# A recurrence with gates over 2,048 tokens: inner products of keys and queries formed per head in a stage of their own and laid out by DMAs

## The reference

```python
def step(St, inp):
    kt, qt, vt, at, bt = inp
    Sk = jnp.einsum('bhij,bhj->bhi', St, kt)
    err = Sk - vt
    Sn = at[..., None] * St - (bt[..., None] * err)[..., None] * kt[:, :, None, :]
    ot = jnp.einsum('bhij,bhj->bhi', Sn, qt)
    return (Sn, ot)
_, outs = jax.lax.scan(step, S0, (tfirst(k), tfirst(q), tfirst(v), tfirst(a), beta.transpose(1, 0, 2)))
```

## Time and profile before

| what | value |
|---|---|
| median of 3 runs | 9,737.57 us |
| lowest, highest | 9,728.86, 9,740.81 us |
| the profiled execution's own time | 9,730.12 us |
| its span, first to last instruction | 9,728.3 us |
| PE busy, share of the span | 7,968.3 us, 82% |
| PEld busy | 4,939.8 us, 51% |
| DVE busy | 5,028.8 us, 52% |
| ACT busy | 2,588.3 us, 27% |
| POOL busy | 2,232.0 us, 23% |
| mean granted clock of PE | 0.687 of full speed |

### The profile page before, as it was taken

The page is one execution under the profiler, slowest core; times in us unless marked ns, Lnnn a source line. Parts: engine busy times, 40 slices in busy tenths (PEclk is TensorE's granted clock), DMA queues, the critical chain, the costliest instruction groups (busy, mean ns, idle before and its releaser), DMA issues. The chain is left out here.

```text
span 9728.3 us, 83645 instructions
## 1 busy us (share of the span) xinstructions
PE 7968.3 (82%) x25042; PEld 4939.8 (51%) x25042; DVE 5028.8 (52%) x7386; ACT 2588.3 (27%) x4982; POOL 2232.0 (23%) x1657
## 2 busy tenths in 40 slices
PE   3888598888899898889978989695452888899799
PEld 2766355555555555555544568542221772222387
DVE  3888544444444444444456643226878773333322
ACT  1232222222222222222223421114442113333111
POOL 0545533333333333333311111010000000000011
PEclk6999755555555555555569989896565558888799
DMA  4343322222222222222221110221110221111200
GB/s 144 127 144 130 105 61 61 61 61 61 61 61 61 61 61 61 61 61 61 61 91 61 48 48 26 101 77 44 30 33 7 62 51 39 35 35 27 94 20 30
DMA packets 635607, 612.38 MB, mean 63 GB/s; under 512 B 457888, under 2 KB 537248, under 8 KB 594080
## 3 DMA queue, kind: packets, MB, share of 16 engines
q1 hardware_dynamic: 635408, 610.13, 21.7%
HBM read 447.65 MB, written 162.40 MB: 63 GB/s over the span
## 5 line engine op out<-in xcount | busy, mean ns | idle before, releaser
L1349 PEld LDWEIGHTS scan_pq<-scan_ring,scan_Ssb 128*128 128x128 f32 x4064 | 911.6, 330 | 296.1 <-issue 296.1
L887 POOL TENSOR_TENSOR ffn_hid_low<-ffn_hid,ffn_hid_high 128x512 fp32r<-128x512 f32 x128 | 164.6, 1286 | 3561.5 <-ACT ffn_hid_high L877 3561.5
L1349 PE MATMUL scan_pq<-scan_ring,scan_Ssb 128*128 128x32 f32 x4064 | 931.8, 399 | 0.0
L297 PE MATMUL proj_acc<-proj_xn,proj_w 128*128 128x512 f32 x3072 | 728.9, 400 | 125.1 <-ACT proj_decay L343 90.9
L2242 PE MATMUL attend_ot<-attend_e,attend_v 128*64 128x512 f32 (+3 forms) x1280 | 679.3, 620 | 91.7 <-ACT attend_e L2269 91.7
L297 PEld LDWEIGHTS proj_acc<-proj_xn,proj_w 128*128 128x128 f32 x3072 | 593.7, 194 | 260.4 <-ACT proj_decay L343 93.8
L1866 PE MATMUL csum_sc<-csum_qk 96*128 96x512 f32 (+3 forms) x640 | 288.4, 567 | 395.5 <-ACT csum_e L1890 350.1
L390 DVE SCALAR_TENSOR_TENSOR proj_y<-proj_raw,proj_cw,proj_y 128x2048 f32<-128x2048 f32 x144 | 574.6, 3990 | 19.1 <-DVE proj_y L386 2.6
L1206 ACT ACTIVATE scan_uT<-scan_turn 64x128 f32<-64x128 f32 x384 | 104.1, 271 | 1698.8 <-PE scan_turn L1360 1698.8
L1254 PE MATMUL scan_work<-scan_gram,scan_ones 128*128 128x512 f32 x512 | 523.1, 1125 | 34.2 <-ACT scan_kT L1220 29.4
L1421 POOL TENSOR_TENSOR scan_gram<-scan_ring,scan_gram 128x512 f32<-128x512 f32 x64 | 96.8, 1513 | 1873.7 <-ACT scan_gram L1161 1873.7
(11 more groups left out here) (238 smaller groups left out, 15730.3 us busy)
## 6 DMA issues: line engine op xcount, KB each, us to landing
scan_abar<-decays SPq DMA_DIRECT2D x128, 1024.0 KB, 4.7
csum_qk<-qk SPq DMA_DIRECT2D x96, 256.0 KB
cmax_qk<-qk SPq DMA_DIRECT2D x96, 256.0 KB
attend_qk<-qk SPq DMA_DIRECT2D x96, 256.0 KB
proj_beta_rows<-beta SPq DMA_DIRECT2D x16, 1024.0 KB, 8.2
stream_k<-proj_res SPq DMA_DIRECT2D x16, 1024.0 KB, 3.9
stream_beta_k<-proj_resb SPq DMA_DIRECT2D x16, 1024.0 KB, 3.9
stream_beta_v<-proj_resb SPq DMA_DIRECT2D x16, 1024.0 KB, 3.8
```

The source lines that it names most:

```text
L297: mm = pe.matmul(acc[:, (j * TT + t) % 8, :], w[:, u, wh, j, k, :], xn[:, xh, k, t * TOK:(t + 1) * TOK], start=(p == 0 and k == 0), stop=( ...
L887: pool.tensor_tensor(hid_low[:, x % 2, :], hid[:, x % 2, :], hid_high[:, x % 2, :].bitcast(F32), ALU.subtract).then_inc(low_done, 1)
L1349: last = pe.matmul(pq[:, nu % 2, :, h, :], Ssb[:, q, g, e, :], ring[:, 0:2, h, nu * C:(nu + 1) * C], start=(q == 0 and g == 0 and e == 0), ...
```

## The change

A new stage, gram_phase, runs between block_decay_phase and scan_phase. For each head it multiplies, with the contraction over the 128 key dimensions, each window of 128 tokens of KK with the same window and the 16 tokens behind it of KB and QQ (288 columns), and turns the window of KK. ACT and VectorE copy the results to SBUF, and SP stores the diagonal parts (16 rows each) to `band` and the turned keys to `kT_dram` in HBM. It also writes zeros into three small tensors in HBM, `xz`, `uz` and `dots`.

In the scan, gram_next, turn_k, gram_first, gram_rest, the eight ones matmuls, their copies and masks are taken out, and so are the seven staging products on GpSimd. In their place SP packs from `band`: pack_dots writes the products inside subblocks to `dots` (28 DMAs per chunk), and build writes those inside a block to `uz` and those across blocks to `xz` (24 DMAs per chunk), each at its place of a matrix that is otherwise zero. load_dots, load_grams and load_keys bring them to SBUF. ACT negates the part of dots that belongs to KB (negate), in block v = 0 of each chunk. The decays are no longer in the ring but in `avec`, one buffer; dots has one buffer too. oring now holds pairs of blocks and is stored every second block. pq is ordered by head, then KB or QQ.

The updates are 128, 256 and 128 columns wide: update 0 reaches only the second subblock; update 1 reaches the third and fourth and carries the first two subblocks' results together (128 rows, the first one scaled by carry_first); update 2 as before.

The diff, cut to the new functions and the order of the work:

```diff
+def gram_phase(nc, streams, band, kT_dram, padded, ident, T):
+    W = T // P
+    SPAN = P + C
+    with ExitStack() as ctx:
+        m = Memory(nc, ctx, "gram")
+        keys = m.sb("keys", [P, 2, T])
+        both = m.sb("both", [P, 2, 2, T + C])
+        tile = m.sb("tile", [P, 2, W, GH + 1, 2, C])
+        kt = m.sb("kt", [P, 2, W, P])
+        zero = m.sb("zero", [P, 2048])
+        idt = m.sb("ident", [P, P])
+        g_ps = m.ps("g", [P, 2, 2, 512])
+        t_ps = m.ps("t", [P, 2, 4, P])
...
+    def load(h, u):
+        one = lambda s: streams[s][bass.ds(h, 1)].rearrange("o p t -> p (o t)")
+        sp.dma_start(keys[:, u, :], one(KK)).then_inc(k_in[u], 16)
+        sp.dma_start(both[:, u, 0, 0:T], one(KB)).then_inc(both_in[u], 16)
+        sp.dma_start(both[:, u, 1, 0:T], one(QQ)).then_inc(both_in[u], 16)
+    def store(i, u):
+        h = i * 2 + u
+        sp.wait_ge(gram_even, (h + 1) * (W // 2))
+        sp.wait_ge(gram_odd, (h + 1) * (W // 2))
+        rows = band[bass.ds(h, 1)].rearrange("o b s w r x -> b s (o w) (r x)")
+        for k in range(GH):
+            sp.dma_start(rows[k], tile[C * k:C * (k + 1), u, :, k:k + 2].rearrange("p w r q t -> p w (r q t)")).then_inc(band_out[u], 16)
+        sp.wait_ge(turn_copied, (h + 1) * TURNS)
+        keys_by_block = kT_dram.rearrange("(w k g) p j -> k (g p) w j", k=GH, g=2)
+        for k in range(GH):
+            sp.dma_start(keys_by_block[k, bass.ds(h * C, C)], kt[C * k:C * (k + 1), u]).then_inc(kt_out[u], 16)
+    sp.dma_start(idt[:, :], ident).then_inc(ident_in, 16)
+    load(0, 0)
+    load(1, 1)
+    sp.wait_ge(zeroed, 3)
+    for flat in padded:
+        sp.dma_start(flat, zero[:, 0:flat.shape[1]]).then_inc(padded_out, 16)
+    def turn(i, more):
+        for u in range(2):
+            store(i, u)
+            if more:
+                load(i * 2 + u + 2, u)
+    run_all(sp, H // 2, turn)
...
+            for w in range(W):
+                if not (isinstance(i, int) and i == 0 and u == 0 and w < 4):
+                    n = h * (W // 2) + w // 2
+                    if w % 2 == 0:
+                        pe.wait_ge(gram_even, n - 1)
+                    else:
+                        pe.wait_ge(gram_odd, n - 1)
+                pe.matmul(g_ps[:, w % 2, (w // 2) % 2, 0:2 * SPAN].rearrange("p (q t) -> p q t", q=2), keys[:, u, w * P:(w + 1) * P],
+                          both[:, u, :, w * P:w * P + SPAN], start=True, stop=True).then_inc(gram_done, 1)
+                if w % 4 == 3:
+                    g = h * TURNS + w // 4
+                    if not (isinstance(i, int) and i == 0 and u == 0 and w // 4 < 2):
+                        pe.wait_ge(turn_copied, g - 1)
+                    for v in range(w - 3, w + 1):
+                        last = pe.transpose(t_ps[:, (w // 4) % 2, v % 4, :], keys[:, u, v * P:(v + 1) * P], idt[:, :])
+                    last.then_inc(turn_done, 1)
+    run_turns(pe, H // 2, turn)
...
+            for w in range(0, W, 2):
+                act.wait_ge(gram_done, h * W + w + 1)
+                act.activation(tile[:, u, w].rearrange("p r q t -> p q r t"),
+                               g_ps[:, 0, (w // 2) % 2, 0:2 * SPAN].rearrange("p (q r t) -> p q r t", q=2, t=C),
+                               ACT.Copy).then_inc(gram_even, 1)
+                if w % 4 == 2:
+                    act.wait_ge(turn_done, h * TURNS + w // 4 + 1)
+                    act.activation(kt[:, u, w - 2:w + 2], t_ps[:, (w // 4) % 2], ACT.Copy).then_inc(turn_copied, 1)
+    run_turns(act, H // 2, turn)
...
+            for w in range(1, W, 2):
+                dve.wait_ge(gram_done, h * W + w + 1)
+                dve.tensor_copy(tile[:, u, w].rearrange("p r q t -> p q r t"),
+                                g_ps[:, 1, (w // 2) % 2, 0:2 * SPAN].rearrange("p (q r t) -> p q r t", q=2, t=C)
+                                ).then_inc(gram_odd, 1)
+    run_turns(dve, H // 2, turn)
...
+    def load_kq(it, half):
+        for w in (RK, RQ):
+            load(w, it, half, kq_in[half])
+    def load_a(it, half):
+        sp.dma_start(avec[:, :, :, :].rearrange("p h n s -> p h (n s)"),
+                     streams[3][:, :, bass.ds(it * RING + half * CHUNK, CHUNK)]
+                     .rearrange("h p t -> p h t")).then_inc(a_in, 16)
+    def pack_dots(it, half):
+        for v in range(BPC):
+            at0 = band[:, BPC * half + v, 0, bass.ds(it, 1), 0]
+            for q, row in ((1, 0), (1, 1), (1, 2), (1, 3), (0, 0), (0, 1), (0, 2)):
+                first = row + 1 - q
+                n = 4 - first
+                place = 4 * row if q else 13 + 3 * row
+                rows = bass.AP(band.tensor, at0.offset + row * TROW + q * C + first, [[HROW, H], [4 * TROW + 4, 4], [1, n]])
+                out = bass.AP(dots.tensor, half * DOTS * U + (4 * v) * DOTS + place, [[SPC * DOTS, H], [DOTS, 4], [1, n]])
+                sp.dma_start(out, rows, allow_slow_non_contiguous=n == 1).then_inc(packed[half], 16)
+    def load_dots(it, half):
+        sp.wait_ge(packed[half], 16 * 7 * BPC * (it + 1))
+        sp.dma_start(gram[:, :, :].rearrange("p u x -> p (u x)"), dots[half:half + 1, :].to_broadcast([P, DOTS * U])).then_inc(dots_in, 16)
+    def build(it, half):
+        for v in range(BPC):
+            rows = band[:, BPC * half + v, :, bass.ds(it, 1)].rearrange("h s o r x -> h (s o) r x")
+            zbase = (half * BPC + v) * XZ
+            sp.dma_start(bass.AP(xz.tensor, zbase, [[C * 256 + 2 * C, H], [256, C], [1, 2 * C]]), rows[:, :, 1, :]).then_inc(built[half], 16)
+            ubase = (half * BPC + v) * P * 512
+            for q in range(2):
+                sp.dma_start(bass.AP(uz.tensor, ubase + q * C + 4, [[4 * 512 + 32, H], [512, 4], [1, 12]]),
+                             rows[:, 0:4, 0, q * C + 4:(q + 1) * C]).then_inc(built[half], 16)
+                sp.dma_start(bass.AP(uz.tensor, ubase + q * C, [[4 * 512 + 32, H], [512, 4], [1, 4]]),
+                             rows[:, 8:12, 0, q * C + 12:(q + 1) * C]).then_inc(built[half], 16)
+            sp.dma_start(bass.AP(uz.tensor, ubase + 64 * 512, [[4 * 512 + 32, H], [512, 4], [1, 32]]),
+                         rows[:, 4:8, 0, :]).then_inc(built[half], 16)
+    def load_keys(it, half):
+        sp.dma_start(kT[:, half].rearrange("p v g j -> p (v g) j"),
+                     kT_dram[bass.ds((2 * it + half) * 2 * BPC, 2 * BPC)].rearrange("n p j -> p n j")).then_inc(kt_in[half], 16)
+    def load_grams(it, half):
+        sp.wait_ge(built[half], 16 * 6 * BPC * (it + 1))
+        for v in range(BPC):
+            zbase = (half * BPC + v) * XZ
+            sp.dma_start(cross[:, half, v], bass.AP(xz.tensor, zbase, [[256, P], [XZ // 2, 2], [1, 256]])).then_inc(grams_in[half], 16)
+        sp.dma_start(inner[:, half].rearrange("p v h t -> p v (h t)"),
+                     uz[half].rearrange("v p x -> p v x")).then_inc(grams_in[half], 16)
+    def store(it, u):
+        sp.wait_ge(o_reduced, it * BPR + u + 1)
+        sp.dma_start(o_dram[:, :, bass.ds(it * RING + (u - 1) * C, 2 * C)].rearrange("h p t -> p h t"),
+                     oring[:, u // 2 % 2]).then_inc(o_stored[u // 2 % 2], 16)
...
+    load_a(0, 0)
+    load_kq(0, 0)
+    pack_dots(0, 0)
+    load_dots(0, 0)
+    build(0, 0)
+    load_keys(0, 0)
+    load_grams(0, 0)
+    load(RV, 0, 0, vb_in[0])
     load_abar(0)
+    load_kq(0, 1)
+    load(RV, 0, 1, vb_in[1])
+    pack_dots(0, 1)
+    build(0, 1)
+    sp.wait_ge(pre_done, 1)
+    load_a(0, 1)
+    load_dots(0, 1)
...
             if u % BPC == BPC - 1 and more:
                 sp.wait_ge(x_done, NSUB * b + 1)
-                load_kqa(it + 1, half)
+                load_kq(it + 1, half)
+            if u % BPC == 0 and (more or half == 0):
+                if not is_zero(b):
+                    sp.wait_ge(ds_done, 4 * b)
+                following = (it, 1) if half == 0 else (it + 1, 0)
+                load_keys(*following)
+                load_grams(*following)
+            if u % BPC == 1 and more:
+                sp.wait_ge(dots_in, 16 * (2 * it + half + 1))
+                pack_dots(it + 1, half)
+            if u % BPC == 2 and more:
+                sp.wait_ge(grams_in[half], 16 * 5 * (it + 1))
+                build(it + 1, half)
             if more or u < BPR - 1:
                 sp.wait_ge(s_decayed, 4 * (b + 1))
                 load_abar(b + 1)
+            if u % BPC == BPC - 1 and more:
+                sp.wait_ge(pre_done, 2 * it + half + 2)
+                load_a(it + 1, half)
+                load_dots(it + 1, half)
+            if u % 2 == 1:
+                store(it, u)
             if u % BPC == BPC - 1:
-                store(it, half)
                 if more:
                     sp.wait_ge(r_done, NSUB * (b + 1))
-                    load(VB, it + 1, half, vb_in[half])
-    with sp.Fori(0, TURNS - 1) as it:
+                    load(RV, it + 1, half, vb_in[half])
+    turn(0, True)
...
+    def negate(c):
+        act.wait_ge(dots_in, 16 * (c + 1))
```

(60 more changed lines are left out.)

353 lines of the change are left out of this document (151 added, 202 removed).

## The result

The changed kernel takes 9,578 us (median of four runs, 9,560 to 9,593) where the kernel before takes 9,733: ratio 0.984 (95% interval in brackets here and below: [0.982, 0.986]), faster by 1.6%. The forecast was 8,990, and the result lies above its range, 8,620 to 9,420. Its profiled execution has a span of 9,557.9 us, 170 less than before.

A forecast was written before the change was run, and what follows sets the result against it. PE's order was taken to bound the scan. Block - 1,449, dots wait + 333, new stage + 350 and scan start + 20 gave - 746 against 9,730.1: 8,984, stated as 8,990 us, range 8,620 to 9,420.

The forecast's parts named there:

- The block's chain: In the scan, PE's order in one block was to take 18.6 us instead of 30.01; 1,449 us leave in all.
- All four removals: In each scan block PE loses gram_next (1.87 us), the turn of the keys (1.23), gram_first (1.47) and gram_rest (1.47).
- the narrower update: Update 0 of each scan block, 128 wide instead of 384, takes 0.73 us instead of 1.57, so 0.84 less.
- Clock: PE's clock in the scan stays at 0.50, the 1.2 GHz level; a rise, giving 8,530 us, had 4 in 100.
- dots: In each chunk's first block, ACT's negate waits for the dots load, landing at carry + 18.1 us; 333 us back in all.
- The negate: On ACT in each chunk's first block: 2.3 us taken, from a range of 1.0 to 3.6, ending at carry + 20.4.
- Stage: The new stage before the scan adds 350 us (290 to 445), and nothing hides it.
- Start of the scan: Chunk 0 needs pack, dots, negate and build in a row: 20 us more (0 to 60).
- The added carry_first (64 elements) and the removed masks lie in its idle time: On VectorE in the scan's blocks: the added instruction and removed masks were to fit its idle time.
- GpSimd's preparation: In each chunk it loses seven staging products, starts its second half after negate, and stays hidden with 15 us to spare.
- small transfer: SP issues 52 more DMAs per chunk, 28 packing and 24 building, at 0.5 us each; cost nothing at that price.
- Rival (b): SP or the queue is late with abar; at c = 1.0 us per small DMA, 381 us lost, 9,370; 17 in 100.

## Why the prediction was wrong

**The block's chain was right.** 18.60 us forecast; 18.52 at v = 2 here, and 18.44 where nothing else is late. All four removals and the narrower update are there, over the 127 intervals 20 us better than forecast if 18.44 is taken as the base. **Clock, dots:** right as forecast; v = 0 blocks cost 321 us above the base for 333. The negate took 1.70 us for the 2.3 taken; the lower end given for it, 1.0 as half of scaled, was a slip, since half of 2.04 x 1,792 / 1,024 is 1.8. **Stage:** 316 for 350. **Start of the scan:** 34 for 20; ACT waits for the dots until 1465.58, some 36 us after the scan's first instruction.

**The step that failed** is "The added carry_first (64 elements) and the removed masks lie in its idle time". Its size was right, 0.22 us, and VectorE had that much idle time. But the instruction has both inputs in SBUF, and it was put into a stretch in which GpSimd works without a break, so it was held there for 20.8 us. The v = 1 blocks took 564 us more than the base: (37.19 - 18.44) x 30 = 562.5, and 1.6 in the others. That is nearly the whole of the 607 us by which the blocks missed. The Trainium skill names the cause: "SBUF — State Buffer", Who interferes with whom, says that VectorE and GpSimd share one pair of ports, and that a VectorE instruction with two SBUF inputs contends for it with a GpSimd instruction that reads SBUF. Which operands count agrees with the runs: only carry_first and the scaling of UB, VectorE's two instructions of the scan with two SBUF inputs, were ever held. That the cause is a port is the page's word; no run here shows it apart from the operands. Its section "SBUF: two separate sides" adds that whichever starts first has the pair for the whole instruction. By that an estimate would have been at most the longest of GpSimd's instructions, 3 us, once per chunk, 90 us. The runs show both: waits to the end of one instruction, and holds that outlast 13 more, 20.6 us.

The kernel before had a sign of it. Its scaling of UB has two SBUF inputs as well:

```profile
L1640 DVE TENSOR_TENSOR scan_UB<-scan_ud,scan_suffix x127: 346/350/1393, 1186.6 to 4986.5; 128x192 f32<-128x192 f32 x127
```

62 of the 127 stood beside a GpSimd instruction. 61 of them took 0.52 to 0.76 us, to the end of that instruction of 0.9 to 1.0 us, and the first took 1.39. None was held further. The prediction also said of GpSimd's preparation that it is hidden: its own length is, but it had become one string of 32 us without a pause in each chunk, where the longest of the kernel before, with its waits for the staged products, was 17.9 us in a steady chunk. That is the other half of the failed step: the run without carry_first still had UB held for 13.2 us in each chunk.

**SP, smaller.** The prediction took 0.5 us for a small transfer; it is 0.74 from one to the next, of which the issue alone takes 0.55. By the prediction's own formula building (24 x 0.74 = 17.7) would just be hidden, but the first of them is held 4.2 us behind abar and the stores, so abar comes late: 72 us in the v = 3 blocks. Packing's lateness (28 x 0.74 = 20.7, against 18.2) was under the hold and showed when that was gone. Rival (b) had the mechanism, with a fifth of its price at c = 1.0.

So 8,984 + 564 + 72 + 3 - 12 - 20 (blocks) - 34 (stage) + 14 (start) - 11 (later stages) = 9,560, the profiled execution's own.

## What to carry to other kernels

When an instruction is added to VectorE, ask where its inputs lie and what GpSimd does at that time: with two inputs in SBUF, beside a string of GpSimd instructions, 64 elements cost 20.8 us. The time shows as VectorE's work, so look for a maximum far above the median. Put one input into PSUM, or let GpSimd wait for the VectorE instruction at a few places; either gave back 5% here. And price a stall in the order in which stalls end: the same move of the negate was worth 124 us while another wait stood behind it and 257 when that was gone, and each wait removed uncovered the next in SP's single queue.
